# Attention with a mixture layer behind it: the normalised input of a batch's later groups goes through DRAM and is turned on VectorE, one group ahead

## The chip, the cores and the metric

The kernel runs on one core of one Trainium2 chip. The metric is the time on the device of one execution, in microseconds (us); the kernel before has a median of 1635.58 us over 3 runs. The core's engines each work through an instruction stream of their own, in order, and meet at semaphores: TensorE (PE, matrix products and transposes into PSUM), VectorE (DVE), ScalarE (ACT), GpSimd (POOL) and SyncE (SP, which here only issues DMAs). An engine that waits holds up all that stands behind the wait in its stream.

## The reference

Four batches of 2048 tokens of width 512, in float32. Attention with a layer norm of its own in front, a residual, a second layer norm, then a mixture layer and a third norm:

```
xn   = layernorm(x) * gamma + beta                    # per token
q, k, v = xn @ Wq, xn @ Wk, xn @ Wv                   # 512 x 512 each
p    = softmax(causal(q @ k.T / sqrt(512)))
x1   = layernorm(x + (p @ v @ Wo + x))
gates = the two largest of softmax(x1 @ wr.T), over their sum      # 8 experts
out[i] += gate * h      # h = silu(silu(x1 @ w1.T) @ w3.T) @ w2.T, added at rows 0 to 7
out  = layernorm(x1 + out)
```

## The kernel before

The weights are folded first: M = Wq·Wkᵀ and Wv·Wo, so that scores are (xn·M)·xnᵀ and the output projection is gone. Every product is made of three float32r products (hi·hi, lo·hi, hi·lo, in `split_product`, lines 351 to 353), which is why each operand exists twice, as `..._hi` (rounded by a copy) and `..._lo` (the rest, a subtraction on DVE).

A batch has 16 tiles of 128 tokens in 4 groups of 4 tiles. For tile t, PE computes the scores of tile t+1 against all keys so far (in chunks of 512 keys, one PSUM bank each), turns the probabilities of tile t, and multiplies them with V (`attend`). ACT takes the exponentials and rounds; DVE takes the maxima and the `lo` halves. In tiles 8 to 14 the probabilities are turned by way of DRAM: SP stores them (`store_p`) and loads them back 32 x 32 blocks at a time (`load_p`, four DMAs of 32 partitions each), and DVE finishes the turn inside the blocks. At the end of the third tile of a group (t % 4 = 2) PE projects the next group: V of its first tile, then G = xn·M (`project_g`), then V of its other three tiles. From the last tile of a batch on, the four loops run over into tile 0 of the next batch; the loop body goes from tile 7 of one batch to tile 6 of the next (`PEELED` = 7).

**The input.** Rows of x are loaded two tiles at a time (a pair) into one buffer `xin`, by ACT's queue; DVE takes their statistics (`norm_x`), POOL makes scale and shift of them, ACT applies these in place. PE then turns them: `turn_x(b, g, u)`, four units u a group, four 128 x 128 transposes each (line 1262). ACT applies gamma and beta on the way out of PSUM (`affine`, line 625), DVE makes `xt_hi` and `xt_lo` (`split_x`, lines 915 and 917). For groups 1 to 3 the units stand in the group before: u = 0 and 1 in its first tile, u = 2 and 3 in its third; for group 0 they stand in tiles 14 and 15 of the batch before.

**The token buffers.** `tok` has 4 slots. SP loads the rows of tile t for the residual; POOL doubles them, DVE adds the attention (`residual`), then two norms follow (`norm_behind`): ACT normalises tile t (x1), SP stores it (`store_x1(t)`, line 421), and only when that store has landed does ACT normalise the slot a second time in place; SP stores that to the output (`store_out`, line 425), and the slot is free for the load of tile t+4. The second normalisation of tile t-1 stands in ACT's stream right behind the first one of tile t, in these lines of `norm_behind`:

```
slot = (t - 1) % SLOTS
act.wait_ge(x1_stored[slot], (b * USES + (t - 1) // SLOTS + 1) * DMA)
y = tok[:, slot, :]
normalise(1, y, y).then_inc(out_ready, 1)
```

`norm_behind(b, 0)`, which stands at the end of ACT's tile 1, thus waits for the store of tile 15 of the batch before. SP's step t, in order: load `tok` of tile t; store and load probabilities (tiles 8 to 14); `store_x1(t-2)`; `store_out(t-3)`.

Of the kernel before, what the change touches and what calls it, by code (L numbers as in the profile page):

```python
# [30 lines left out]
P = 128  # L31
D = 512
# [8 lines left out]
def attention_mlp(nc, x, wq_t, wk_t, wv_t, wo, gamma, beta, w1_t, w3_t, w2_t, wr_t, out):  # L41
# [32 lines left out]
    x1_scratch = nc.dram_tensor("x1_scratch", [B * S, D], F32, kind="Internal").ap()  # L74

    with ExitStack() as whole:
# [44 lines left out]
        rinv = sb("rinv", [P, 2], F32, stage01)  # L121
        xt_hi = sb("xt_hi", [P, DC, S], F32R, stage01)
# [46 lines left out]
        x_loaded = [sem(f"x_loaded{i}") for i in range(2)]  # L169
        x_normed = sem("x_normed")  # L170
        x_turned = sem("x_turned")
# [210 lines left out]

        block = whole.enter_context(nc.Block())
# [9 lines left out]
        def _(sp):  # L393
            for s in start_at_one:
                sp.sem_inc(s, 1)
            weights = [w.rearrange("(c p) n -> p c n", p=P) for w in (wq_t, wk_t, wv_t, wo)]
            for pair in range(2):
                for part, c in enumerate(PARTS):
                    for i in (2 * pair, 2 * pair + 1):
                        sp.dma_start(raw[i][:, c, :], weights[i][:, c, :]).then_inc(weights_loaded[i][part], DMA)  # L400
                if pair == 0:
                    sp.dma_start(gamma_sb[:], gamma).then_inc(affine_loaded, DMA)
                    sp.dma_start(beta_sb[:], beta).then_inc(affine_loaded, DMA)
# [22 lines left out]

            def tile(b, t, before=True, last=False):
# [3 lines left out]
                sp.dma_start(tok[:, slot, :], x[bass.ds(b * S + t * P, P), :]).then_inc(res_loaded[slot], DMA)  # L431
                if t in FAR:
# [17 lines left out]
                if t in FAR:  # L450
                    for c in range(2, chunks(t)):
                        load_p(b, t, c)

            for t in range(3):
                tile(0, t, before=False)
            with sp.Fori(0, B - 1) as b:
                for t in range(3, TILES):
                    tile(b, t)
                for t in range(3):
                    tile(b + 1, t)  # L460
            for t in range(3, TILES):
# [27 lines left out]
        def _(pool):  # L489
# [26 lines left out]
            def norm_x(b, pair):  # L516
                n = b * PAIRS + pair
# [11 lines left out]
            def tile(b, t, last=False, before=True):  # L529
# [5 lines left out]
                if k == 3 and g + 2 < GROUPS:  # L535
                    norm_x(b, 2 * (g + 2))
                if k == 3 and g + 2 == GROUPS and not last:
                    norm_x(b + 1, 0)
# [8 lines left out]
                if t == TILES - 1 and not last:  # L547
                    norm_x(b + 1, 2)
                if k == 0 and g + 1 < GROUPS:
                    norm_x(b, 2 * (g + 1) + 1)  # L550
# [8 lines left out]
            for pair in range(FIRST_PAIRS):  # L559
                norm_x(0, pair)  # L560
# [40 lines left out]
        def _(act):  # L601
# [12 lines left out]
            def load_x(b, pair):  # L614
                for slot in range(2):
                    act.dma_start(xin[:, slot, :], x[bass.ds(b * S + (2 * pair + slot) * P, P), :]).then_inc(x_loaded[slot], DMA)

            def turn_x(b, g, u, more=True):

                n = g * XUNITS + u  # L620
                act.wait_ge(xt_ready, 1 + b * (GROUPS * XUNITS) + n)
                act.wait_ge(x_turned, b * (GROUPS * XUNITS) + n + 1)
# [5 lines left out]
                if u % 2 == 1 and more:  # L628

                    if n // 2 + 1 < TILES // 2:  # L630
                        load_x(b, n // 2 + 1)
                    else:
                        load_x(b + 1, 0)
# [9 lines left out]
            def norm_x(b, pair):  # L643
                act.wait_ge(x_shift, b * PAIRS + pair + 1)
                normalise(2, xin[:, 0, :], xin[:, 0, :])
                normalise(3, xin[:, 1, :], xin[:, 1, :]).then_inc(x_normed, 1)
# [62 lines left out]
            def tile(b, t, last=False, before=True):  # L709
# [5 lines left out]
                if more and k == 0:  # L715
                    turn_x(b, g + 1, 0)
                if chunks(t) > 1:
                    turn_probs(b, t, 1)
                if more and k == 0:
                    turn_x(b, g + 1, 1)  # L720
                if more and k == 2:
                    turn_x(b, g + 1, 2)
# [8 lines left out]
                if more and k == 1:  # L731
                    norm_x(b, 2 * (g + 1) + 1)
                for c in range(max(chunks(t), n_next)):
                    if c >= 2 and c < chunks(t):
                        turn_probs(b, t, c)
                    if more and k == 2 and c == chunks(t) - 1:
                        turn_x(b, g + 1, 3, more=not (last and g + 2 == GROUPS))
# [6 lines left out]
                    if c == 1 and t == TILES - 2 and not last:  # L744
                        turn_x(b + 1, 0, 1)
                    if c == 1 and t == TILES - 1 and not last:
                        turn_x(b + 1, 0, 3)
                    if c == 2 and t == TILES - 1 and not last:
                        project_g(b + 1, 0)
                if t == TILES - 2:  # L750
                    turn_probs(b, TILES - 1, 0)
                if k == 3 and g + 2 < GROUPS:
                    norm_x(b, 2 * (g + 2))
                if k == 3 and g + 2 == GROUPS and not last:
                    norm_x(b + 1, 0)
# [4 lines left out]
                if more and k == 2:  # L760
                    project_v(b, GROUP * (g + 1))
                    project_g(b, g + 1)
                    for j in range(1, GROUP):
                        project_v(b, GROUP * (g + 1) + j)
                if t == TILES - 1 and not last:
                    exp_first(b)
                    norm_x(b + 1, 2)
# [22 lines left out]
            load_x(0, 0)  # L790
            weights_to_hi(0, range(1))
            norm_x(0, 0)
            weights_to_hi(0, range(1, 2))
            act.wait_ge(affine_loaded, 2 * DMA)
            turn_x(0, 0, 0)
            weights_to_hi(0, range(2, 3))
            turn_x(0, 0, 1)
# [3 lines left out]
            norm_x(0, 1)  # L801
            turn_x(0, 0, 2)
            turn_x(0, 0, 3)
# [3 lines left out]
            norm_x(0, 2)  # L807
# [55 lines left out]
        def _(dve):  # L863
# [40 lines left out]
            def norm_x(b, pair):  # L904
                for s in range(2):
# [620 lines left out]
```

## Time and profile before

| | |
|---|---|
| median of 3 runs | 1635.58 us (1634.55 to 1635.96) |
| the profiled execution, its time | 1635.72 us |
| its span in the profile | 1633.9 us |
| busy: PE, DVE, ACT, POOL | 99%, 54%, 42%, 17% |
| granted TensorE clock | 1.00 throughout |
| DMA: SP's queue, ACT's queue | 28.5% and 3.6% of 16 engines' span |

How to read it: PE is the engine that counts, and its busy share is nearly the whole span, so time comes off only where PE has less to do, and goes on where something makes PE wait. The busy time of a group of PE instructions is the union of overlapping intervals; what one instruction costs is better read from the distance of the starts around it. Attention takes the first 1180 us or so, the mixture layer the rest; the change touches attention alone.

### The profile page before, as it was taken

How to read it: one execution, taken by the hardware profiler on the slowest of the kernel's cores; microseconds unless marked ns; L12 is line 12 of the kernel's file. 1: busy time of each engine (PE TensorE's matmuls, PEld its weight loads, DVE VectorE, ACT ScalarE, POOL GpSimd, SP SyncE). 2: the span in 40 equal slices, each digit the busy share in tenths (PEclk: the TensorE clock that was granted, in tenths of full speed). 3: DMA queues.
4: the chain of work that ended last, by engine and by line, in shares of the span. 5: the costliest groups of instructions: out<-in, count | busy, mean ns of one | idle time of the engine just before them, and what ended most of it. 6: DMA issues, size and time to landing. Idle time of an engine off the chain costs nothing.

```text
span 1633.9 us, 23601 instructions
## 1 busy us (share of the span) xinstructions
PE 1615.7 (99%) x7591; PEld 1335.6 (82%) x7591; DVE 885.7 (54%) x2296; ACT 681.0 (42%) x1301; POOL 283.8 (17%) x491
## 2 busy tenths in 40 slices
PE   9999999999999999999999999999999999999998
PEld 7888888888888888888888888888878888888886
DVE  5564645565364555455455545545565656556563
ACT  5443433353343344343333434343344444444442
POOL 1120201121120112121101212010131221212211
PEclk9999999999999999999999999999999999999999
DMA  4111625321154432123535123253664313223100
GB/s 161 59 61 52 155 76 139 100 94 56 60 136 104 113 94 95 54 91 107 134 85 123 61 76 104 78 138 97 157 133 63 51 26 51 37 40 51 26 0 8
DMA packets 365766, 136.64 MB, mean 84 GB/s; under 512 B 317008, under 2 KB 321104, under 8 KB 365664
## 3 DMA queue, kind: packets, MB, share of 16 engines
q1 hardware_dynamic: 354768, 116.48, 28.5%
q10 hardware_dynamic: 10896, 18.90, 3.6%
q8 instruction: 53, 0.87, 0.2%
q14 instruction: 49, 0.40, 0.1%
HBM read 79.73 MB, written 55.59 MB: 83 GB/s over the span
## 4 chain that ended last, share of the span: by engine, by line
PE 80%; issue 10%; DVE 4%; ACT 2%; POOL 2%; DMA 1%; ACTq 0%; POOLq 0%; SPq 0%; DVEq 0%
PE psum L351 25%; PE psum L353 25%; PE psum L352 25%; PE psum L1326 1%; PE psum L1262 1%; PE psum L1437 1%; PE psum L1436 1%; POOL rstd L512 1%; PE psum L1445 1%; PE psum L1444 1%; DVE pt_lo L934 1%; ACT affine L625 1%; ACT tok L641 0%; DMA raw<-in_wk_t 0%; DVE xt_hi L915 0%
## 5 line engine op out<-in xcount | busy, mean ns | idle before, releaser
L351 PE MATMUL psum<-xt_hi,g_hi 128*128 128x512 f32 (+3 forms) x640 | 237.5, 371 | 0.4 <-DVE g_lo L923 0.4
L353 PE MATMUL psum<-xt_lo,g_hi 128*128 128x512 f32 (+3 forms) x640 | 229.6, 359 | 0.0
L352 PE MATMUL psum<-xt_hi,g_lo 128*128 128x512 f32 (+3 forms) x640 | 229.3, 358 | 0.0
L351 PE MATMUL psum<-v_hi,pt_hi 128*128 128x512 f32 x544 | 220.8, 406 | 6.2 <-DVE pt_lo L934 3.9
L353 PE MATMUL psum<-v_lo,pt_hi 128*128 128x512 f32 x544 | 212.8, 391 | 0.0
L352 PE MATMUL psum<-v_hi,pt_lo 128*128 128x512 f32 x544 | 212.7, 391 | 0.0
L509 POOL TENSOR_TENSOR var_eps<-meanvar,eps 128x2 f32<-128x2 f32 (+1 forms) x97 | 18.9, 195 | 1005.4 <-DVE meanvar L901 1004.3
L946 DVE TENSOR_REDUCE rowmax<-psum 128x1 f32<-128x512 f32 (+3 forms) x160 | 97.1, 608 | 149.1 <-PE psum L353 147.7
L820 ACT ACTIVATE act_f<-psum 128x512 f32<-128x512 f32 x128 | 76.7, 599 | 199.7 <-PE psum L353 199.1
L641 ACT ACTIVATE tok<-tok,shift,rstd 128x512 f32<-128x512 f32 x128 | 97.5, 809 | 104.1 <-POOL shift L514 103.8
L590 POOL TENSOR_TENSOR expo<-euler,shifted 128x32 f32<-128x32 f32 x16 | 86.9, 5429 | 282.1 <-DVE shifted L1163 282.1
L696 ACT ACTIVATE pt_hi<-pt_f 128x512 fp32r<-128x512 f32 (+2 forms) x96 | 55.4, 578 | 191.0 <-DVE pt_f L942 190.4
L351 PEld LDWEIGHTS psum<-xt_hi,g_hi 128*128 128x128 f32 x640 | 121.1, 189 | 17.1 <-issue 0.7
L352 PEld LDWEIGHTS psum<-xt_hi,g_lo 128*128 128x128 f32 x640 | 120.7, 189 | 15.9
L353 PEld LDWEIGHTS psum<-xt_lo,g_hi 128*128 128x128 f32 x640 | 120.3, 188 | 15.9
L351 PEld LDWEIGHTS psum<-v_hi,pt_hi 128*128 128x128 f32 x544 | 102.2, 188 | 34.6 <-DVE pt_lo L934 11.3
L353 PEld LDWEIGHTS psum<-v_lo,pt_hi 128*128 128x128 f32 x544 | 102.2, 188 | 22.6
L352 PEld LDWEIGHTS psum<-v_hi,pt_lo 128*128 128x128 f32 x544 | 102.4, 188 | 18.3
L679 ACT ACTIVATE probs<-psum,bias 128x512 f32<-128x512 f32 (+3 forms) x157 | 97.1, 623 | 28.5 <-DVE bias L953 12.4
L927 DVE TENSOR_TENSOR v_lo<-psum,v_hi 128x512 fp32r<-128x512 f32 x64 | 44.1, 689 | 119.5 <-ACT v_hi L663 119.5
L923 DVE TENSOR_TENSOR g_lo<-psum,g_hi 128x512 fp32r<-128x512 f32 x64 | 44.3, 692 | 118.7 <-ACT g_hi L638 118.7
L351 PE MATMUL psum<-wvo_hi,h_hi 128*128 128x512 f32 x256 | 101.7, 397 | 2.0 <-DVE h_lo L1153 2.0
(149 smaller groups left out, 3400.6 us busy)
## 6 DMA issues: line engine op xcount, KB each, us to landing
xin<-in_x ACTq DMA_DIRECT2D x64, 256.0 KB, 2.8
tok<-in_x SPq DMA_DIRECT2D x64, 256.0 KB, 2.7
x_scratch<-tok SPq DMA_DIRECT2D x64, 256.0 KB, 2.2
out_dram<-tok SPq DMA_DIRECT2D x64, 256.0 KB, 2.3
p_scratch<-probs SPq DMA_DIRECT2D x64, 256.0 KB, 2.0
probs<-p_scratch SPq DMA_DIRECT2D x256, 64.0 KB, 2.5
x_in<-x_scratch SPq DMA_DIRECT2D x64, 256.0 KB, 4.3
p_scratch<-probs SPq DMA_DIRECT2D x16, 192.0 KB, 1.9
```

The lines of the kernel that those rows point to most:

```text
L351: pe.matmul(o, ws, ms, start=first, stop=False, skip_group_check=True)
L352: pe.matmul(o, w_lo, ms, start=False, stop=False, skip_group_check=True)
L353: return pe.matmul(o, ws, m_lo_, start=False, stop=last, skip_group_check=True)
L509: pool.tensor_tensor(var_eps[:, a:z], meanvar[:, a:z, 1], eps[:, o], ALU.add).then_inc(rooted, 1)
L590: pool.tensor_tensor(expo[:], euler[:], shifted[:], ALU.pow).then_inc(exp_ready, 1)
L641: return act.activation(o, y, ACT.Identity, bias=shift[:, slot:slot + 1], scale=rstd[:, slot:slot + 1])
L679: act.activation(probs[:, at:at + w], psum[:, c, 0:w], ACT.Exp, bias=bias[:, t % 2:t % 2 + 1], scale=SCALE, accum_out=sums4[:, t % 2, c:c ...
L696: act.activation(pt_hi[:, n % 2, 0:w], turned_, ACT.Copy).then_inc(pt_hi_ready, 1)
L820: act.activation(act_f[:, n % 2, :], psum[:, bank, :], ACT.Silu)
L923: dve.tensor_tensor(g_lo[:, j, :], psum[:, j, :], g_hi[:, j, :], ALU.subtract).then_inc(g_ready, 1)
L927: dve.tensor_tensor(v_lo[:, tile, :], psum[:, turn_bank(v_use(tile)), :], v_hi[:, tile, :], ALU.subtract).then_inc(v_ready, 1)
L946: return dve.tensor_reduce((rowmax if chunks(t) == 1 else rowmax4)[:, c:c + 1], psum[:, c, 0:width(t, c)], AX.X, ALU.max)
```

## The change

For groups 1 to 3 of batches 1 to 3, and for group 3 of the first batch (`in_dram`), PE no longer turns the input. ACT normalises a pair in place as before; SP stores the pair to a new DRAM buffer (`store_xn`), and one group ahead loads the whole group back in 32 x 32 blocks (`load_xq`: 16 DMAs of 32 partitions and 64 KB, four for each of the four blocks of 128 columns) into the memory of `xt_lo`, seen as unrounded floats (`xt_b`). DVE turns it inside the blocks into the memory of `xt_hi` (`turn_xq`, four transposes of 128 x 512), ACT applies gamma and beta into `xt_b` (`affine_x`), DVE makes `xt_hi` and `xt_lo` in place (`split_xq`). This stands under the projection of the group in front, between the `lo` half of its first V tile and those of G; for group 1 it stands in tile 15 of the batch before. The loads of group 2 stand in SP's step 1, those of group 3 at the end of step 5, those of the next batch's group 1 in step 15. The pairs of a batch are now normalised in the order 2, 3, 4, 0, 1, 5, 6, 7, mostly loaded by SP; in the first batch pairs 6 and 7 are loaded behind the weights into `xt_a`. Group 0, and groups 1 and 2 of the first batch, are turned by PE as before.

```
+        def in_dram(first, g):
+            return g >= (FIRST_PE_GROUPS if first else 1)        # FIRST_PE_GROUPS = 3
+            def store_xn(b, pair, first=False):
+                sp.wait_ge(x_normed, normed_before(b, pair, first) + 1)
+                sp.dma_start(pair_rows(xn_scratch, b, pair), x_pair(pair, first)).then_inc(xn_stored, DMA)
+            def next_pair(b, pair, behind):
+                sp.wait_ge(xn_stored, stored_with(b, behind) * DMA)
+                load_pair(sp, b, pair)
+            def load_xq(b, g):
+                rows_of = xn_scratch[bass.ds(b * S + g * (GROUP * P), GROUP * P), :].rearrange("(t j) (c q i) -> q j c t i", j=LANES, q=QUADRANTS, i=LANES)
+                for c in range(DC):
+                    for q in range(QUADRANTS):
+                        sp.dma_start(xt_b[q * LANES:(q + 1) * LANES, c, columns(g)].rearrange("j (t i) -> j t i", i=LANES),
+                                     rows_of[q][:, c]).then_inc(xq_loaded[g], DMA)
             def tile(b, t, before=True, last=False):                        # SP
                 sp.wait_ge(out_stored[slot], 1 + (b * USES + t // SLOTS) * DMA)
                 sp.dma_start(tok[:, slot, :], x[bass.ds(b * S + t * P, P), :]).then_inc(res_loaded[slot], DMA)
+                if t < PEELED and before:
+                    if t == 0:
+                        store_xn(b, 5)
+                    if t == 1:
+                        next_pair(b, 6, behind=5)
+                        load_xq(b, 2)
...
+                    if t == TILES - 1:
+                        sp.wait_ge(scores_ready, b * CHUNKS + CHUNKS)
+                        load_xq(b + 1, 1)
...
                 elif before:
                     store_x1(b - 1, TILES + t - 2)
...
+                if t == 5:
+                    sp.wait_ge(xn_stored, stored_with(b, 7) * DMA)
+                    load_xq(b, 3)
...
+            def affine_x(b, g, c):                                          # ACT
+                act.wait_ge(xq_turned, dram_groups_before(b, g) * DC + c + 1)
+                act.activation(xt_b[:, c, columns(g)], xt_a[:, c, columns(g)],
+                               ACT.Identity, bias=beta_sb[:, c:c + 1], scale=gamma_sb[:, c:c + 1]).then_inc(affine_ready, 1)
...
+            def turn_xq(b, g, c):                                           # DVE
+                dve.wait_ge(xq_loaded[g], (b + 1 if g == GROUPS - 1 else b) * (DC * LOADS))
+                dve.transpose(xt_a[:, c, columns(g)], xt_b[:, c, columns(g)]).then_inc(xq_turned, 1)
+            def split_xq(b, g, c):
+                n = (b * GROUPS + g) * XUNITS + c + 1
+                dve.wait_ge(affine_ready, 1 + n)
+                dve.tensor_copy(xt_hi[:, c, columns(g)], xt_b[:, c, columns(g)]).then_inc(xt_hi_ready, 1)
+                dve.wait_ge(xt_hi_ready, n)
+                dve.tensor_tensor(xt_lo[:, c, columns(g)], xt_b[:, c, columns(g)], xt_hi[:, c, columns(g)],
+                                  ALU.subtract).then_inc(xt_ready, 1)
...
                 if more and k == 2:                                         # DVE, end of a group's third tile
-                    split_x(b, g + 1, 3)
                     split_v(b, GROUP * (g + 1))
+                    if g + 2 < GROUPS and in_dram(not before, g + 2):
+                        for part in range(DC):
+                            turn_xq(b, g + 2, part)
+                        for part in range(DC):
+                            split_xq(b, g + 2, part)
                     split_g(b, g + 1)
```

Three places where the streams now read otherwise. The first is SP's step 1 of a later batch: the load of `tok` for tile 1, the store of x1 of tile 15 of the batch before, its `out` store of tile 14, and the wait for tile 2's slot. Before:

```order
L431 ISA [waits out_stored1]
L431 DMA tok<-in_x 128x512
L420 REGISTER_ALU
L421 DMA x_scratch<-tok 128x512 [waits x1_ready]
L425 DMA out_dram<-tok 128x512 [waits out_ready]
L431 ISA [waits out_stored2]
```

The same step now; the rows left out repeat the two of `xt_b` until there are 16 DMAs:

```order
L523 DMA tok<-in_x 128x512 [waits out_stored1]
L508 ISA
L435 ISA [waits xn_stored]
L435 DMA xin<-in_x 128x512
L435 ISA
L435 DMA xin<-in_x 128x512
L516 DMA xt_b<-xn_scratch 32x16x32
L516 ISA
...
L516 DMA xt_b<-xn_scratch 32x16x32
L496 REGISTER_ALU
L497 DMA x_scratch<-tok 128x512 [waits x1_ready]
L501 DMA out_dram<-tok 128x512 [waits out_ready]
```

Two loads of a pair and 16 block loads have come between the load of tile 1 and the store of x1 of tile 15.

The second is ACT from the end of tile 1 into tile 2 of a later batch: the first normalisation of tile 0, the second of tile 15 of the batch before, and the rounding of tile 2's turned probabilities (`pt_hi`), which PE's `attend` of tile 2 needs. Before:

```order
L641 ACTIVATE tok<-tok,shift,rstd 128x512 [waits shift_ready]
L657 ISA
L641 ACTIVATE tok<-tok,shift,rstd 128x512 [waits x1_stored3]
L693 REGISTER_ALU [waits probs_turned]
L696 ACTIVATE pt_hi<-psum 128x384 [waits pv_done]
L621 REGISTER_ALU
L625 ACTIVATE affine<-psum,beta_sb,gamma_sb 128x256 [waits x_turned,xt_ready]
```

And now:

```order
L770 ACTIVATE tok<-tok,shift,rstd 128x512 [waits shift_ready]
L787 REGISTER_ALU
L770 ACTIVATE tok<-tok,shift,rstd 128x512 [waits x1_stored3]
L823 REGISTER_ALU [waits probs_turned]
L826 ACTIVATE pt_hi<-psum 128x384 [waits pv_done]
L773 REGISTER_ALU
L770 ACTIVATE xin<-xin,shift,rstd 128x512 [waits x_shift]
```

The order of these is as it was up to `pt_hi`; behind it the `affine` of the input is gone and the normalisation of a pair has come.

The third is DVE at the projection in tile 2 of a later batch. Before:

```order
L927 TENSOR_TENSOR v_lo<-psum,v_hi 128x512 [waits v_hi_ready]
L914 REGISTER_ALU
L915 CAST xt_hi<-affine 128x2x256 [waits affine_ready]
L917 TENSOR_TENSOR xt_lo<-affine,xt_hi 128x2x256 [waits xt_hi_ready]
L927 TENSOR_TENSOR v_lo<-psum,v_hi 128x512 [waits v_hi_ready]
L923 TENSOR_TENSOR g_lo<-psum,g_hi 128x512 [waits g_hi_ready] x4
```

And now, with two more pairs of CAST and TENSOR_TENSOR in the rows left out:

```order
L1083 TENSOR_TENSOR v_lo<-psum,v_hi 128x512 [waits v_hi_ready] x2
L1055 STREAM_TRANSPOSE xt_a<-xt_b 128x512 [waits xq_loaded2] x4
L1059 ISA
L1060 CAST xt_hi<-xt_b 128x512 [waits affine_ready]
L1061 REGISTER_ALU
L1062 TENSOR_TENSOR xt_lo<-xt_b,xt_hi 128x512 [waits xt_hi_ready]
...
L1062 TENSOR_TENSOR xt_lo<-xt_b,xt_hi 128x512 [waits xt_hi_ready]
L1079 TENSOR_TENSOR g_lo<-psum,g_hi 128x512 [waits g_hi_ready]
```

Four transposes and four pairs of copy and subtraction now stand between V of the group's first tile and the `lo` half of G.

## Rows read from the trace of the kernel before

**Rows 1.** The page, part 1: busy time, share of span, instructions.
```profile
PE 1615.7 (99%) x7591; PEld 1335.6 (82%) x7591; DVE 885.7 (54%) x2296; ACT 681.0 (42%) x1301; POOL 283.8 (17%) x491
```

**Rows 2.** Grouped instructions, by form: op, tiles, count | busy us, mean ns | idle before.
```profile
L1262 PE MATMUL psum<-ident,xin 128*128 128x128 f32 x256 | 38.6, 273 | 1.5 <-ACT affine L625 1.0
...
L942 DVE STREAM_TRANSPOSE pt_f<-probs 128x512 f32<-128x512 f32 x64 | 45.1, 705 | 9.0 <-PE psum L353 9.0
L917 DVE TENSOR_TENSOR xt_lo<-affine,xt_hi 128x512 fp32r<-128x512 f32 x64 | 44.3, 692 | 2.2
...
L915 DVE CAST xt_hi<-affine 128x512 fp32r<-128x512 f32 x64 | 28.6, 447 | 24.0 <-ACT affine L625 23.7
```

**Rows 3.** Timeline of PE, tile 10: start us, us, line, op, [idle before].
```profile
203.00 0.60 PE L1262 MATMUL psum<-ident,xin 128*128 128x128 f32 x4
...
203.67 0.40 PE L352 MATMUL psum<-v_hi,pt_lo 128*128 128x512 f32 x1
203.90 0.40 PE L353 MATMUL psum<-v_lo,pt_hi 128*128 128x512 f32 x1
```

**Rows 4.** Timeline of PE, batch 1, tile 2: the turn, and attend.
```profile
354.81 0.55 PE L1326 MATMUL psum<-ident,probs 128*128 128x128 f32 x3 [0.15 <-ACT probs L679]
...
361.67 0.48 PE L351 MATMUL psum<-v_hi,pt_hi 128*128 128x512 f32 x1
```

**Rows 5.** Timeline of SP's DMA issues, batch 1, steps 0 and 1.
```profile
347.49 0.33 SPq L421 DMA_DIRECT2D x_scratch<-tok  x1
348.19 0.33 SPq L425 DMA_DIRECT2D out_dram<-tok  x1
350.34 0.35 SPq L431 DMA_DIRECT2D tok<-in_x  x1
351.49 0.33 SPq L421 DMA_DIRECT2D x_scratch<-tok  x1
```

**Rows 6.** Timeline of ACT, batch 1: norms in tiles 0 and 1.
```profile
346.66 1.51 ACT L641 ACTIVATE tok<-tok,shift,rstd 128x512 f32<-128x512 f32 x2
...
356.99 1.52 ACT L641 ACTIVATE tok<-tok,shift,rstd 128x512 f32<-128x512 f32 x2 [1.75 <-POOL shift L514]
```

**Rows 7.** Timeline of DVE, batch 1: tile 1's maximum, tile 2's probabilities.
```profile
344.65 0.42 DVE L946 TENSOR_REDUCE rowmax<-psum 128x1 f32<-128x256 f32 x1
...
358.91 0.56 DVE L934 TENSOR_TENSOR pt_lo<-psum,pt_hi 128x384 fp32r<-128x384 f32 x1 [2.20 <-ACT pt_hi L696]
```

**Rows 8.** Timeline of SP: eight block loads of 64 KB, four of 256 KB.
```profile
457.52 5.34 SPq L416 DMA_DIRECT2D probs<-p_scratch  x8
...
1183.27 5.11 SPq L361 DMA_DIRECT2D x_in<-x_scratch  x4
```

**Rows 9.** The page, part 6: DMA issues, KB each, us from issue to landing.
```profile
x_scratch<-tok SPq DMA_DIRECT2D x64, 256.0 KB, 2.2
...
probs<-p_scratch SPq DMA_DIRECT2D x256, 64.0 KB, 2.5
...
w_sb<-in_w_t SPq DMA_DIRECT2D x1, 1024.0 KB, 5.6
```

**Rows 10.** Timeline of DVE: idle in tile 15 (first two rows) and tile 6.
```profile
322.01 0.43 DVE L915 CAST xt_hi<-affine 128x512 fp32r<-128x512 f32 x1 [2.54 <-ACT affine L625]
...
328.30 0.69 DVE L923 TENSOR_TENSOR g_lo<-psum,g_hi 128x512 fp32r<-128x512 f32 x1 [3.08 <-ACT g_hi L638]
...
435.05 0.69 DVE L923 TENSOR_TENSOR g_lo<-psum,g_hi 128x512 fp32r<-128x512 f32 x1 [6.11 <-ACT g_hi L638]
```

**Rows 11.** Timeline of SP, batch 0: step 15 begins.
```profile
300.00 0.46 SPq L431 DMA_DIRECT2D tok<-in_x  x1
```

**Rows 12.** Stretch behind PE's last product: us, busy by engine (count), clock, DMA.
```profile
1629.00:1633.90 4.90, 0.00 (x0) 0.00 (x0) 2.20 (x5) 0.00 (x0) 0.55 (x1) 1.00 0.02 3
```

**Rows 13.** Grouped instructions of PE: products on the identity, early and late.
```profile
L1401 PE MATMUL psum<-ident 128*128 128x128 f32 x28 | 5.2, 368 | 2.3 <-POOL mask_bf L498 2.3
L1428 PE MATMUL psum<-ident 128*128 128x128 f32 x40 | 4.9, 277 | 0.1
```

More of the change, by code:

```diff
@@ L534, in tile @@
                 pool.tensor_tensor(y, y, y, ALU.add).then_inc(res_doubled, 1)
[L535 to L538, printed above, removed]
+                slot = pair_at(b, t, not before, last)
+                if slot and t in AT_MIDDLE:
+                    norm_x(*slot)
                 if t == TILES - 2 and not last:
@@ L559, in _ @@
             for pair in range(FIRST_PAIRS):
-                norm_x(0, pair)
+                norm_x(0, pair, first=True)
             for t in range(PEELED):
@@ L612, in fold_to_hi, with turn_x @@
                     act.activation((m_hi, wvo_hi)[pair][:, n % DC, :], psum[:, fold_bank(n), :], ACT.Copy).then_inc(fold_hi, 1)
[L614 to L622, printed above, removed]
+            def turn_x(b, g, u, first=False, then_load=None):
+                act.wait_ge(xt_ready, 1 + b * (GROUPS * XUNITS) + g * XUNITS + u)
+                act.wait_ge(x_turned, turned_before(b, g, u, first) + 1)
                 for k in range(2):
@@ L714, in tile @@
                     turn_probs(b, t, 0)
[L715 to L716 removed]
+                on_pe = not before and not in_dram(True, g + 1)
+                if on_pe and k == 0:
+                    turn_x(b, g + 1, 0, first=True)
                 if chunks(t) > 1:
                     turn_probs(b, t, 1)
[L719 to L722, printed above, removed]
+                if on_pe and k == 0:
+                    turn_x(b, g + 1, 1, first=True, then_load=2 * (g + 1) + 1)
+                if on_pe and k == 2:
+                    turn_x(b, g + 1, 2, first=True)
                 if t == TILES - 2 and not last:
@@ L730, in tile @@
                     norm_behind(b, t - 2)
-                if more and k == 1:
-                    norm_x(b, 2 * (g + 1) + 1)
+                slot = pair_at(b, t - 1, not before, last) if t else None
+                if slot and t - 1 in AT_END:
+                    norm_x(*slot)
                 for c in range(max(chunks(t), n_next)):
@@ L735, in tile @@
                         turn_probs(b, t, c)
-                    if more and k == 2 and c == chunks(t) - 1:
-                        turn_x(b, g + 1, 3, more=not (last and g + 2 == GROUPS))
+                    if on_pe and k == 2 and c == chunks(t) - 1:
+                        turn_x(b, g + 1, 3, first=True, then_load=2 * (g + 2) if g + 2 < FIRST_PE_GROUPS else None)
                     if c < n_next:
@@ L751, in tile @@
                     turn_probs(b, TILES - 1, 0)
[L752 to L755, printed above, removed]
+                slot = pair_at(b, t, not before, last)
+                if slot and t in AT_MIDDLE:
+                    norm_x(*slot)
                 if t and t < TILES - 2:
@@ L998, in tile @@
                     turn_probs(b, t, 1)
-                if more and k == 0:
+                on_pe = not before and not in_dram(True, g + 1)
+                slot = pair_at(b, t, not before, last)
+                if on_pe and k == 0:
                     split_x(b, g + 1, 0)
@@ L1036, in tile @@
                 if t == TILES - 1 and not last:
+                    for part in range(DC):
+                        turn_xq(b + 1, 1, part)
                     split_x(b + 1, 0, 3)
@@ L1049, in tile @@
                     split_probs(b, t, 3)
+                if t == TILES - 1 and not last:
+                    split_xq(b + 1, 1, 2)
+                    split_xq(b + 1, 1, 3)
                 if t == TILES - 2:
@@ L1055, in tile @@
                     split_wr()
+                if on_pe and k == 2:
+                    split_x(b, g + 1, 3)
                 if more and k == 2:
-                    split_x(b, g + 1, 3)
                     split_v(b, GROUP * (g + 1))
+                    if slot and t in AT_PROJECTION:
+                        norm_x(*slot)
+                    if g + 2 < GROUPS and in_dram(not before, g + 2):
+                        for part in range(DC):
+                            turn_xq(b, g + 2, part)
+                        for part in range(DC):
+                            split_xq(b, g + 2, part)
                     split_g(b, g + 1)
```

212 lines of the change are left out of this document (153 added, 59 removed).

## The prediction

> **What bounds the kernel now.** I read the page's first part first: PE is busy 99% of the span and no other engine over 54% [rows 1]. So a change pays by what it takes from PE's stream and costs by the time for which it makes PE wait; work on DVE, ACT or the DMA queues costs nothing until PE waits for it. Then the grouped instructions, for the operation that goes [rows 2]; then the timelines of PE, SP, ACT and DVE at the places where the new work lands, to see what waits last there. The second step decides this case: it is not the transposes that cost, nor the work that replaces them, but a store that ends up behind the new loads on SP.
>
> **What is removed from PE.** The transposes of the input come as 256 instructions [rows 2], 64 units of four. In the timeline a unit starts at 203.00 and the second product behind it at 203.67, where two products behind each other are 0.23 apart (203.67 to 203.90) [rows 3]: a unit costs 0.67 - 0.23 = 0.44 us. Ten groups leave PE (group 3 of the first batch, groups 1 to 3 of three batches), four units each: 40 x 0.44 = 17.6 us. PE also waits 0.15 us for ACT at 354.81 [rows 4], behind a pair's normalisation that is no longer in ACT's tile 1; three batches, 0.5 us. Gross gain 18.1 us.
>
> **What takes its place on DVE and ACT.** A group needs four transposes (0.705 each), four copies (0.447) and four subtractions (0.692) [rows 2], 7.4 us of DVE. In tiles 2 and 6 they stand under the projection, where DVE idles 6.11 us before the first part of G [rows 10]. The copies wait for ACT's four `affine_x`, at 0.76 us each as in ACT's norms [rows 6], which start one transpose later and stay ahead of DVE. So the first part of G is 1 to 2 us late on DVE; the next parts catch up (0.69 us of work every 1.36 us), and PE needs G only behind three V tiles, 36 products of 0.23, 8 us. Cost 0. Were that cover gone, each microsecond over 8 would cost three to seven in the whole. In tile 15 the transposes (2.8 us) fall into the 2.54 us of idle before 322.01 and two of the splits into the 3.08 us before 328.30 [rows 10]; PE works on the first half of G there. Cost 0 to 0.5 us in all; I take 0.
>
> **Whether the loads are there in time.** SP is done with tile 14 at 300.00 [rows 11], and the last scores have run. Sixteen loads of 64 KB follow. The nearest row is the block load of the probabilities, of the same shape: eight take SP 5.34 us, 0.667 each [rows 8], and land 2.5 us after issue [rows 9]. So group 1's loads take 10.7 us and are there by about 314; for the transposes to end by 322.0 DVE must begin at 319: 5 us to spare. The loads of step 5 have a whole tile to spare.
>
> **What the loads delay: the term that decides.** In step 1 the 16 loads stand ahead of `store_x1` of tile 15. ACT's stream ends tile 1 with the second normalisation of tile 15, which waits for that store to land; behind it stands `pt_hi` of tile 2, behind that on DVE `pt_lo`, and PE's `attend` of tile 2 waits for that. Before, the store is issued at 351.49 [rows 5], lands 2.2 us later [rows 9], and ACT asks at 356.99 [rows 6]: nobody waits. Now, on the axis of batch 1:
> - DVE's maximum for tile 1 at 344.65 [rows 7] stood behind two splits of the input; without them, and with PE's unit gone, it comes about 1.0 us sooner; ACT is rid of two pairs of `affine` and two DMA issues. I put the norm of 346.66 [rows 6] at 344.7, 2.0 sooner, and with it the three issues of [rows 5]: the output store at 346.2, the load of tile 1, which waits 2.15 us for it, at 348.4.
> - Two loads of a pair: the first block load at 349.4 to 349.6.
> - 16 x 0.667 = 10.7 us, and up to 0.75 each, 12.0 us, for the register instruction ahead of each: the store issued at 360.2 to 361.6.
> - It lands 2.2 us later; ACT's second normalisation takes half of 1.52, 0.76; from the end of that pair (356.99 + 1.52 = 358.51) to the end of `pt_lo` (358.91 + 0.56 = 359.47) are 0.96 [rows 6, 7]; I add 0.15 for PE to start. Sum 4.1: 364.3 to 365.7.
> - PE would be there at 361.67 [rows 4] less four units and the wait, 1.9: 359.75.
>
> So PE waits 4.5 to 5.9 us, three times. The middle, 5.2, leaves out that the store's packets go behind block loads; I take 5.4: 16.2 us. Behind it nothing more is late: the delayed V halves, `exp` and the load of tile 2 have the projection's 22 us (96 products of 0.23). Step 5 puts the same loads ahead of `store_x1` of tile 4, which ACT needs only at the end of its tile 6, when two tiles' scores have passed: 0; if they were too short, each microsecond short would cost four. In step 15 the stores behind the loads wait for a norm in the middle of tile 15 anyway: 0. The bounds for this term: nothing (if SP gets through its 16 issues in under 6 us) to 3 x 8 (issues of 0.83).
>
> **The rest.** In the first batch two loads of 512 KB go behind the weights; a load of 1 MB lands in 5.6 us [rows 9], and ACT's second pair shares the engines with it: 0 to 3 us, I take 0.5. The pair stores and loads at SP's steps 8 to 12 add about 1 us to a step; the stores of probabilities behind them wait for ACT's exponentials that long: 0 to 1, I take 0.
>
> **The sum.** The profiled execution took 1635.7 us (the median of the runs is 1635.6). 1635.7 - 18.1 + 16.2 + 0.5 + 0 = 1634.3. By its own steps the forecast lies between 1629 and 1640.
>
> **Rivals.**
> 1. *SP gets through the loads quickly.* The x1 loads of the mixture layer move 1 MB with four issues in 5.11 us [rows 8]; if the time goes with the bytes and not with the issues, the 16 take 5.1 us, the store lands before 357, and PE waits for nothing: 1635.7 - 18.1 + 0.5 = 1618. Against it: the row of equal shape has 0.667 for 64 KB. The Trainium skill (DMA: Bandwidth & Descriptors, section "Issuing engines are not separate DMA queues") says the sequencer's time to start a DMA is usually small beside the DMA itself. By that rule the answer would be this rival's; the trace does not agree here, where 0.667 us an issue stands against 2.5 us to landing, and 16 issues are four times a landing.
> 2. *The wait also costs PE its clock* (the one on the slower side). If a wait of over 5 us lets TensorE fall to its lower level, PE starts `attend` of tile 2 slow. The price from rows: the program's first 14 products on the identity (28 records), after an idle start, took 5.2 us, and 20 of them late in the program (40 records) 4.9 us [rows 13]; 14 at the late rate are 3.4, so 1.8 us a time, 5.4 in three: 1639.7. It decides from the point where the wait outlasts what the clock holds. For it: the length. Against it: behind PE's last product the granted clock stays 1.00 over 4.90 us without one [rows 12], and the waits are only somewhat longer. The Trainium skill (TensorE: Matmul & The Clock Gate, section "What's actually happening") has activity as what releases the lower clock of 1.2 GHz and idleness as what brings it back; the row shows no fall within its 4.90 us.
> 3. *The block loads are slow*, at 1 us an issue, because 16 behind each other fill the queue: PE then waits 11 us in tile 2, and the loads of tile 15 land at 319, just in time: 1635.7 - 18.1 + 3 x 10.7 + 0.5 = 1650. Eight and even twelve such loads in one step do not slow down now, which speaks against it.
>
> **Chances.** Forecast 0.47, rival 1 0.18, rival 2 0.25, rival 3 and what I have not seen 0.10. A difference of less than about 0.2%, 3.3 us (1632.3 to 1638.9), is what a measurement of this kernel cannot tell from no change. The forecast's own spread of 5 us to both sides gives it about 0.13 faster, 0.29 the same, 0.05 slower; rival 1 is 0.18 faster; rival 2 0.08 the same and 0.17 slower; rival 3 0.02 the same and 0.08 slower. Together 0.31 faster, 0.39 the same, 0.30 slower. The range reaches from just over rival 1 to past rival 2: 1619 to 1645.
>
> **What would show it.** Right: in PE's waits three waits of 4 to 7 us before `attend` of tile 2 in batches 1 to 3, for `pt_lo`; ACT idle as long before a normalisation of `tok`, released by the DMA of x1; SP's 16 block loads in 10 to 12 us right before that store; the transposes on the identity down from 256 to 96; no wait of PE for `xt_lo` or `g_lo` at the projections. Wrong: SP through the loads in under 6 us and no wait (rival 1); the clock below 1.00 behind those waits (rival 2); waits in tile 15 or at the projections, which would put the cost in the loads or DVE instead.

## The result and the profile after

The changed kernel takes 1642.46 us (median of 8 runs, 1638.87 to 1648.61) against 1636.14 us before (8 runs, 1634.55 to 1637.51): a ratio of 1.0041, with a 95% interval from 1.0028 to 1.0054. It is slower by 6.3 us. I had forecast 1634.3 us, no change, with a chance of 0.30 for slower. The profiled execution is the slowest of the eight, 1648.61 us, with a mean granted clock of 0.992; the other seven have 0.994 to 0.996 and the kernel before 1.00. The sizes below that rest on the clock are therefore taken from several profiles and from the timed runs, not from this one alone. As an estimate, one less the mean clock, times the span, is the most that the half clock can have cost: 13 us in the profiled run, 7 to 10 in the other seven. In each set of experiments the kernel before was run again (medians 1636.21 to 1636.52), and the ratios are to these runs.

The page's first part and the grouped instructions answer to [rows 1, 2]. The transposes of the input on PE are 96 where 256 were, and the 40 transposes on DVE take 0.679 us each, where 0.705 was forecast:

```profile
PE 1609.1 (98%) x7431; PEld 1329.1 (81%) x7431; DVE 906.6 (55%) x2336; ACT 671.5 (41%) x1261; POOL 280.9 (17%) x491
...
L1433 PE MATMUL psum<-ident,xin 128*128 128x128 f32 x96 | 14.5, 273 | 0.8 <-ACT affine L752 0.8
...
L1055 DVE STREAM_TRANSPOSE xt_a<-xt_b 128x512 f32<-128x512 f32 x40 | 24.8, 679 | 0.0
```

The first thing to look at is what PE waits for (us in total, times, longest). One line has grown. Before:

```profile
PE psum L351 <- DVE pt_lo L934: 3.9, 9, 1.4
```

And now:

```profile
PE psum L360 <- DVE pt_lo L1090: 22.1, 13, 4.0
```

PE's timeline shows where these 22.1 us lie. Three waits stand before `attend` of tile 2 (367.65, and 3.89 and 3.81 us in the next two batches), as the prediction has them, 11.7 us together. Another 6.8 us stand in places that the prediction does not have: in `attend` of tile 9 (191.39, 490.08, 493.53, 787.10) and once in that of tile 8 (776.48); the last batch, which prepares no input, has none of them. (The tile is told by its products, three for each tile of keys: 30 follow in tile 9. The expectations below say tiles 9 and 10.) The other 3.7 us lie in places where the kernel before waits too. There is no new wait at the projections or in tile 15:

```profile
191.39 0.47 PE L360 MATMUL psum<-v_hi,pt_hi 128*128 128x512 f32 x1 [1.96 <-DVE pt_lo L1090]
...
367.65 0.77 PE L360 MATMUL psum<-v_hi,pt_hi 128*128 128x512 f32 x1 [3.97 <-DVE pt_lo L1090]
...
369.06 0.63 PE L360 MATMUL psum<-v_hi,pt_hi 128*128 128x512 f32 x1
...
490.08 0.47 PE L360 MATMUL psum<-v_hi,pt_hi 128*128 128x512 f32 x1 [2.16 <-DVE pt_lo L1090]
```

The row at 369.06 shows a second loss: three products take 1.41 us there (367.65 to 369.06) where 0.69 (3 x 0.23) is what they take elsewhere. The windows around the wait (us; busy us of PE, PEld, DVE, ACT, POOL; granted clock; DMA) show the clock at its lower level behind it:

```profile
360.00:364.00 4.00, 3.67 (x17) 2.68 (x15) 0.44 (x1) 0.08 (x1) 1.12 (x4) 1.00 0.81 128
364.00:368.00 4.00, 0.35 (x1) 0.38 (x2) 1.06 (x2) 2.28 (x4) 0.00 (x0) 0.83 0.51 155
368.00:372.00 4.00, 4.00 (x10) 3.09 (x10) 2.58 (x10) 1.58 (x4) 2.23 (x5) 0.50 0.84 307
372.00:376.00 4.00, 4.00 (x16) 3.18 (x15) 0.00 (x0) 2.06 (x3) 1.09 (x2) 0.81 0.50 145
```

The wait itself is followed back over SP and ACT (they answer to [rows 5, 6]). The store of x1, at 351.49 before, is issued at 363.05, behind 16 block loads; ACT's second normalisation waits 5.65 us for its landing:

```profile
353.02 0.88 SPq L435 DMA_DIRECT2D xin<-in_x  x2
354.00 8.82 SPq L516 DMA_DIRECT2D xt_b<-xn_scratch  x16
363.05 0.38 SPq L497 DMA_DIRECT2D x_scratch<-tok  x1
```

```profile
365.72 0.81 ACT L770 ACTIVATE tok<-tok,shift,rstd 128x512 f32<-128x512 f32 x1 [5.65 <-DMA x_scratch<-tok]
366.44 0.47 ACT L826 ACTIVATE pt_hi<-psum 128x384 fp32r<-128x384 f32 x1
```

The waits of tile 9 begin on SP too. In the kernel before, SP issues the load of `tok` in step 9, waits for ACT's probabilities, stores them, and loads them back from 179.12 on:

```profile
173.10 0.45 SPq L431 DMA_DIRECT2D tok<-in_x  x1
176.69 2.28 SPq L408 DMA_DIRECT2D p_scratch<-probs  x3
179.12 5.37 SPq L416 DMA_DIRECT2D probs<-p_scratch  x8
```

Now SP stands from 176.34 to 180.10 until the stored pair has landed; only then does it issue the next pair's loads and, behind them, the stores of tile 9's probabilities. From the load of `tok` to the first block load are 8.4 us instead of 6.0, and DVE gets the probabilities back too late by the 2.46 us of the last row:

```profile
175.30 0.46 SPq L505 DMA_DIRECT2D xn_scratch<-xin  x1
175.97 0.37 SPq L523 DMA_DIRECT2D tok<-in_x  x1
180.10 0.87 SPq L435 DMA_DIRECT2D xin<-in_x  x2
181.09 1.37 SPq L484 DMA_DIRECT2D p_scratch<-probs  x3
184.40 5.36 SPq L492 DMA_DIRECT2D probs<-p_scratch  x8
```

```profile
189.07 0.71 DVE L1098 STREAM_TRANSPOSE pt_f<-probs 128x512 f32<-128x512 f32 x1 [2.46 <-DMA probs<-p_scratch]
```

In SP's waits the same shows as a new line, 20.0 us in nine waits (steps 3, 9 and 11 of three batches); in DVE's, the wait for the probabilities' loads is 12.8 us in nine where it was 1.1 in one:

```profile
SPq L435 <- DMA xn_scratch<-xin: 20.0, 9, 3.8
```

```profile
DVE pt_f L1098 <- DMA probs<-p_scratch: 12.8, 9, 2.5
```

In step 11 SP waits as long (from 208.28 to 212.10 in the first batch), but PE projects the next group ahead of `attend` of tile 11 and waits for nothing there.

### The profile page after: what moved, and what is told of

It reads as the page before. It is cut to its first block, busy times and chain, and to the rows that moved or that the text cites. A ratio compares the mean times of both kernels' runs of the same rounds, so it can differ in the third digit from the quotient of the medians.

```text
span 1646.8 us, 23816 instructions
## 1 busy us (share of the span) xinstructions
PE 1609.1 (98%) x7431; PEld 1329.1 (81%) x7431; DVE 906.6 (55%) x2336; ACT 671.5 (41%) x1261; POOL 280.9 (17%) x491
## 4 chain that ended last, share of the span: by engine, by line
PE 76%; issue 11%; DMA 3%; DVE 3%; SPq 2%; POOL 2%; ACT 2%; POOLq 0%; DVEq 0%; ACTq 0%
PE psum L360 24%; PE psum L362 24%; PE psum L361 24%; SPq L492 2%; DMA p_scratch<-probs 1%; PE psum L1497 1%; DMA xn_scratch<-xin 1%; POOL rstd L645 1%; PE psum L1610 1%; PE psum L1611 1%; PE psum L1619 1%; PE psum L1618 1%; ACT tok L770 1%; DMA raw<-in_wk_t 1%; PE psum L1433 1%
## 5 line engine op out<-in xcount | busy, mean ns | idle before, releaser
L360 PE MATMUL psum<-v_hi,pt_hi 128*128 128x512 f32 x544 | 222.2, 408 | 25.0 <-DVE pt_lo L1090 22.1
L360 PEld LDWEIGHTS psum<-xt_hi,g_hi 128*128 128x128 f32 x640 | 121.1, 189 | 17.6 <-issue 0.8
L360 PE MATMUL psum<-wvo_hi,xt_hi 128*128 128x512 f32 x256 | 101.0, 395 | 0.0
```

The lines of the kernel that those rows point to most:

```text
L360: pe.matmul(o, ws, ms, start=first, stop=False, skip_group_check=True)
```

## The experiments

The theory after the two traces: the gain on PE is there; it is given back by two orders on SP (block loads ahead of the store of x1 in step 1; a wait for the stored pair ahead of the probabilities in steps 9 and 11), by the granted clock behind the waits, and by 1 to 2 us at the start. The rivals: the pair's loads, not the block loads, are the delay in step 1; contention between the transfers; DVE's new work. Each edit shown below is against the changed kernel.

**Stores first in step 1.**
```
                     if t == 1:
                         next_pair(b, 6, behind=5)
-                        load_xq(b, 2)
...
+                if t == 1 and before:
+                    load_xq(b, 2)
                 if t == 2 and before:
                     store_xn(b, 6)
```


> Alone of the changed kernel: in SP's step 1 the 16 block loads go behind the stores of that step. Theory (the loads ahead of the store of x1 make PE wait, and the clock falls behind the wait): the three waits of 3.8 to 4.0 us before attend of tile 2 go, 11.7 us, and with them three stretches of 6.8 us at half clock, up to 10 us; 1620 to 1626, and a mean granted clock nearer to 1. Rival A (the two loads of a pair and the wait for the stored pair ahead of them are the delay): the waits lose less than 1 us each; 1639 to 1642. Rival B (the loss lies in DVE's work or in the transfers' contention): the waits stay or move; 1638 to 1643.

Measured: 1625.06 us (1623.56 to 1626.5), 0.9928 of before [0.9915, 0.9941], 17.4 us less than with the change as it was. The three waits are gone, and the mean clock is 0.999. What is left of the same line, 7.9 us, lies in tile 9 (0.98, 1.25 and 1.94 us in the three batches) and in places that waited before:

```profile
PE psum L360 <- DVE pt_lo L1091: 7.9, 8, 1.9
```

Neither contention nor DVE's work can be the main loss: the same bytes move and DVE does the same work.

**The pair later.**
```
                     if t == 1:
-                        next_pair(b, 6, behind=5)
+                        sp.wait_ge(xn_stored, stored_with(b, 5) * DMA)
                         load_xq(b, 2)
...
+                if t == 1 and before:
+                    load_pair(sp, b, 6)
```


> Alone of the changed kernel: in SP's step 1 the two loads of a pair go behind the stores of that step; the 16 block loads stay ahead of them. Theory: the store of x1 is about 1 us earlier, the three waits are 2.9 us instead of 3.9; 1637 to 1642, the clock may still fall. Rival A (the pair is the delay): the waits go, 1620 to 1626.

Measured: 1648.07 us (1646.55 to 1651.16), ratio 1.0074 [1.0060, 1.0089]: 5.6 us slower than the change, where I expected 1637 to 1642; neither the theory nor the rival has this. The waits of PE are 5.59, 6.24 and 5.41 us. The store of x1 does come earlier (359.32, 9.0 us behind the start of the step's first issue, the load of `tok`, where it was 10.7), and ACT is done with tile 2's `pt_hi` at 362.80. But now DVE is late: the statistics of pair 6 stand ahead of the residual and of `pt_lo`, and start at 364.37, when the pair's loads, now issued from 360.41 on, have landed (the view names no releaser for this wait):

```profile
364.37 1.29 DVE L1037 BATCH_NORM_STATS2 stats<-xin 128x6 f32<-128x512 f32 x2 [8.11 <-issue]
...
366.49 0.55 DVE L1092 TENSOR_TENSOR pt_lo<-psum,pt_hi 128x384 fp32r<-128x384 f32 x1
```

So two paths from SP's step 1 end in the same wait: over the store and ACT, and over the pair's loads and DVE. The pair's loads were not what delayed the store, but they are not free to go last either. Of the two, only the 16 block loads can go last in step 1.

**Pair loads behind the stores of the probabilities (steps 9 and 11).**
```
-                    if t == 9:
-                        next_pair(b + 1, 3, behind=2)
-                    if t == 11:
-                        next_pair(b + 1, 4, behind=3)
...
                     for c in range(chunks(t)):
                         store_p(b, t, c)
+                    if t in (9, 11) and not last:
+                        next_pair(b + 1, {9: 3, 11: 4}[t], behind={9: 2, 11: 3}[t])
                     for c in range(2):
                         load_p(b, t, c)
```


> Alone of the changed kernel: in SP's steps 9 and 11 the wait for the stored pair and the loads of the next pair go between the stores of the probabilities and their loads. Theory (SP's wait of 4 us holds up the probabilities): PE's waits in tiles 9 and 10 (1.96 us in the first batch, 2.61 in the second, 2.19 in the third) go or fall under 0.5, and the fall of the clock near 192 with them; 1633 to 1638. Rival (the pairs' stores and loads share the DMA engines with the probabilities, whatever the order): the waits stay; 1640 to 1643.

Measured: 1634.08 us (12 runs, 1631.5 to 1638.3), ratio 0.9987 [0.9978, 0.9996], 8.4 us less than the change. No wait over 0.3 us is left in tiles 8 to 10. SP's timeline (to be held against the one from 175.30 above; this run is about 1.3 us earlier by then) shows why. The three stores of probabilities are spread over 3.62 us, because SP waits for ACT between them; by then the pair has landed, and its successor's loads follow without a wait. The eight block loads start at 180.41 instead of 184.40, 2.7 us sooner when the 1.3 are taken off:

```profile
173.98 0.46 SPq L505 DMA_DIRECT2D xn_scratch<-xin  x1
174.65 0.37 SPq L523 DMA_DIRECT2D tok<-in_x  x1
175.49 3.62 SPq L484 DMA_DIRECT2D p_scratch<-probs  x3
179.41 0.88 SPq L435 DMA_DIRECT2D xin<-in_x  x2
180.41 5.34 SPq L492 DMA_DIRECT2D probs<-p_scratch  x8
```

Of SP's nine waits for a stored pair three are left, those of step 3:

```profile
SPq L435 <- DMA xn_scratch<-xin: 1.9, 3, 0.6
```

DVE still waits for the pair (2.59 us at 182.83, where it was 2.26), and PE does not wait for it. The transfers are the same, so contention whatever the order is out as the main loss here as well. In the change the first store of probabilities, right behind the pair's loads, did land late (issued at 181.09, its block loads could start only at 184.40); how much of the wait that made is not separated from SP's own wait.

**All three edits**, with the early loads of the first batch held back behind `sp.wait_ge(x_normed, 2)`.

> Both edits (stores first in step 1; pair loads behind the stores of the probabilities in steps 9 and 11), and the first batch's two early loads of 512 KB held until the second pair of the input is normalised. Theory: the gains add up, 18 to 22 us, 5 to 8 us and 0 to 1.5 us: 1613 to 1620, faster than the kernel before by 1.0 to 1.4%; no PE wait over 1.5 us but those that stand in the kernel before too. Rival (the gain of 17.6 us on PE is not there, because something else replaces the transposes): 1630 to 1636.

Measured: 1616.11 us (1615.39 to 1617.76), ratio 0.9875 [0.9860, 0.9889]: 20 us faster than the kernel before. PE's waits for `pt_lo` are down to what they were before the change (3.9 us in 9):

```profile
PE psum L360 <- DVE pt_lo L1089: 3.7, 5, 1.3
```

**The start.** The held-back loads alone, and the two other edits without them:

> Alone of the changed kernel: the two early loads of 512 KB are held until the second pair of the input is normalised. Theory (they and the longer start delay the weights and the second pair): the first scores start at 45.8 to 46.5 us instead of 48.2; 1639 to 1642. Rival (the start varies from run to run, whatever the loads): first scores at 46.8 to 48.3 as in the kernels with the early loads; 1641 to 1644.

Measured: 1643.01 us (1641.64 to 1644.67), no change; first scores at 47.31 us (the product behind PE's wait for the first `g_lo`). That is the rival's case.

> Stores first in step 1, and pair loads behind the stores of the probabilities in steps 9 and 11, with the early loads where the change put them. Theory: 1 to 2 us over the 1616.1 of the kernel with the early loads held back; 1616 to 1619, first scores at 46.8 to 48.3. Rival (holding back the early loads is worth nothing): 1615 to 1617.

Measured: 1617.91 us (1617.4 to 1618.65), ratio 0.9887 [0.9872, 0.9903]; first scores at 47.32 us. The start is settled in part only. When the first weights let PE begin varies from 7.7 to 9.96 us in all these profiles, whatever the loads. From there to the first scores it takes 38.4 to 39.1 us in seven of the eight profiles with the early loads (48.23 - 9.49 in the change), 40.5 in the eighth, and 37.4 to 38.2 in the three without (45.92 - 7.71 before). So the loads cost about 1 us, too little for the time of a single pair of kernels to show; the difference of 1.8 us between the two last versions, whose intervals overlap, fits it, and the first edit alone does not contradict it.

**The clock.** Ahead of `attend` of tile 2, PE works on the identity while it waits:
```
+                    if t == 2 and before:
+                        for _ in range(14):
+                            pe.matmul(psum[:, XBANK, 0:P], ident[:], ident[:], start=True, stop=True)
                     attend(b, t, c)
```


> Alone of the changed kernel: 14 products on the identity, about 3.4 us, into a bank that nobody reads, ahead of attend of tile 2 in batches 1 to 3, where PE waits 3.9 us anyway. The wait on DVE is not shortened. Theory (the clock falls behind the waits and that costs about 3 us a time): the waits left are about 0.5 us, the granted clock there stays 1.00; 1633 to 1638. Rival (the clock costs nothing beside the wait): no change, 1641 to 1644.

Measured: 1639.9 us (1636.75 to 1645.27), ratio 1.0030 [1.0018, 1.0042]: 2.6 us less than the change, under the 4 to 9 that I expected, and by itself not clear of the noise: the interval overlaps that of the change (1.0028 to 1.0054). PE's waits left behind the idle products are 0.93 to 1.28 us, where I expected 0.5. The clock holds:

```profile
360.00:364.00 4.00, 4.00 (x30) 3.68 (x29) 0.00 (x0) 0.00 (x0) 0.00 (x0) 1.00 0.77 198
364.00:368.00 4.00, 2.99 (x18) 2.50 (x17) 2.20 (x7) 3.87 (x7) 0.00 (x0) 1.00 0.50 133
```

The same on top of the kernel with the pair loads behind the stores of the probabilities, where no other wait blurs it:

> The kernel with the pair loads behind the stores of the probabilities (1634.1 us), with the 14 idle products ahead of attend of tile 2 besides, so that no wait in the far tiles blurs the price of the clock. Theory: of the 16.2 us by which that kernel is slower than the one with the stores first in step 1 as well (1617.9), three waits of 3.6 us are 10.8 and the clock is 5.4; with the clock held 1628 to 1631. Rival (the clock costs nothing beside the waits): 1633 to 1636.

Measured: 1632.6 us (11 runs, 1630.38 to 1635.46), ratio 0.9979 [0.9970, 0.9988]: 1.5 us less than without, short of the 3 to 6 expected, and again with overlapping intervals. The clock did hold in every run: its mean is 0.999 to 1.00 in all 11, where it is 0.994 to 0.997 in the 12 without the idle products. The profiles tell why so little came of it. Without the idle products the clock is low behind the wait:

```profile
362.00:366.00 4.00, 3.85 (x10) 3.07 (x11) 3.08 (x10) 2.08 (x5) 0.00 (x0) 0.57 0.66 232
```

The wait there is 3.56 to 3.64 us and tile 2's batch is 5.2 to 5.4 us longer than with the stores first (first `attend` of tile 15 to the next: 293.25, 293.00 and 291.46 against 287.83, 287.78 and 286.10). From the start of the last product to `attend` are 3.95 to 4.02 us there, 3.7 to 3.8 more than the usual 0.23, which leaves 1.5 to 1.6 us a time for the clock. With the idle products the batches are 4.4 to 5.0 longer, all of it wait: from the first idle product to `attend` are 4.4 to 4.9 us, 0.6 to 1.1 more than the 3.7 to 3.8 without them. In the first two of the three the store of x1 took 1.12 and 1.19 us to issue instead of 0.37, in the third the 16 block loads took 9.95 us instead of 8.84, so the store landed later. The clock's price, 1.5 to 1.6 us a time, is thus read from the profiles; the timed runs agree with it but do not fix it. Why SP was slower with PE busy, or whether that is chance, stays open.

**A quarter of the bytes.** In step 1 each block load is cut in two, a quarter of the rows ahead of the stores, three quarters behind:
```
                     if t == 1:
                         next_pair(b, 6, behind=5)
-                        load_xq(b, 2)
+                        load_xq(b, 2, slice(0, 1))
...
+                if t == 1 and before:
+                    load_xq(b, 2, slice(1, GROUP))
```


> Alone of the changed kernel: in step 1 each of the 16 block loads is cut in two: a quarter of it stays ahead of the store of x1, the other three quarters go behind the stores. 16 issues stay ahead, with a quarter of the bytes. If SP's time goes with the issues (0.55 us each), the waits before attend of tile 2 stay 3.9 us; 1640 to 1644. If it goes with the bytes or the rows, 16 issues take 3 to 6 us, the waits fall to 0 to 1.2 us, the clock holds; 1622 to 1630.

Measured: 1644.1 us (1642.81 to 1645.8), ratio 1.0047 [1.0032, 1.0063]. SP's time goes mainly with the number of issues:

```profile
353.50 7.90 SPq L516 DMA_DIRECT2D xt_b<-xn_scratch  x16
361.63 0.37 SPq L497 DMA_DIRECT2D x_scratch<-tok  x1
...
362.98 9.07 SPq L516 DMA_DIRECT2D xt_b<-xn_scratch  x16
```

16 quarters take 7.90 us, 0.49 each; 16 whole ones 8.82. The waits of tile 2 are 2.40 to 2.47 us, between the two expectations: 0.9 is from the issues, 0.6 because the store lands sooner (ACT has it 2.0 us after its issue, 2.7 in the change), probably for having fewer bytes ahead of it. What that saves comes back at the end of tile 2, where PE waits 1.43 to 2.19 us for `v_lo`. SP's load of `tok` for tile 2 now stands behind the second 16 loads and is issued at 372.24 instead of 366.54; POOL waits for it, ACT's next norm waits for POOL, and behind that norm stands the rounding of V:

```profile
372.24 0.35 SPq L523 DMA_DIRECT2D tok<-in_x  x1
```

```profile
377.61 1.52 ACT L772 ACTIVATE tok<-tok,shift,rstd 128x512 f32<-128x512 f32 x2 [10.07 <-POOL shift L649]
```

## Why the prediction was wrong

Four versions split the loss: 1616.11 (all three edits), 1617.91 (early loads back, +1.8), 1625.06 (pair loads back ahead of the probabilities, +7.2), 1642.46 (block loads back ahead of the store, +17.4). The other way round step 1 is worth 16.2 (1634.08 - 1617.91) and the pair loads 8.4 (1642.46 - 1634.08).

- *The gain on PE, 18.1 us:* about right, 2 us too small. From the first scores to the last batch's tile 15 the kernel before takes 1147.87 us (45.92 to 1193.79), the one with two edits 1127.76 (47.32 to 1175.08): 20.1. The price of a unit holds: in 39 of the 64 units of the kernel before, the second product behind a unit starts 0.67 or 0.68 us after it, as in the one place that I read. Laid side by side, the two PE streams differ by 18.1 us at the 40 units, near the 17.6 forecast; the other 2.0 us lie in many small steps between them, among them 0.3 us three times at the wait for ACT at 354.81, for which I had 0.15.
- *DVE and ACT under the projections and in tile 15, 0 us:* right. PE waits for neither `xt_lo` nor, there, `g_lo`. *The loads of tile 15 and step 5:* right, too.
- *The wait before `attend` of tile 2, 16.2 us:* the place, the chain and the count are right. That the sum is right as well is luck, for it is not made of what I added up. The wait is 3.6 to 4.0 us and not 5.4, because an issue takes SP 0.55 us there and not 0.667 to 0.75 [rows 8] (with the stores first the same 16 loads take 10.94 us, 0.68 each; why the two differ stays open). The rest is the clock, which this term did not have.
- *The clock (rival 2):* its mechanism is what happened, on top of a shorter wait than I had given it. I argued against it from 4.90 us without a fall behind PE's last product [rows 12]; before `attend` of tile 2 it fell with every wait of 3.56 us or more, twelve in four profiles. Its price, 1.8 a time, is near the 1.5 to 1.6 of the kernel with the pair loads moved; in the profile of the change itself it is higher, since the clock is low for longer there (the windows from 364 to 376 show 0.83, 0.50 and 0.81, where the other kernel has one window at 0.57).
- *Rival 1 (the bytes, not the issues):* wrong. The quarters show it. The rule of the Trainium skill that I weighed there (DMA: Bandwidth & Descriptors, section "Issuing engines are not separate DMA queues"), that the sequencer's time for a DMA is usually small beside the transfer, does not help here: 16 times 0.49 to 0.55 us stands ahead of a store that lands in under 3.
- *The pair stores and loads at SP's steps 8 to 12, "0 to 1, I take 0":* this is the step that failed, by 7.2 to 8.4 us. I counted the issues, about 1 us a step, and not the wait for the stored pair's landing ahead of the next pair's loads, 3.8 us at the place shown. My reason for 0, that the stores of probabilities wait for ACT that long, I read off no row. In the kernel before SP does wait there, from 173.55 to 176.69, which would cover the issues but not the wait besides; and in the kernel with the pair loads moved ACT is ready sooner, and SP waits for it only until 175.49, 0.5 us behind the load of `tok`. The 8.4 is the less certain of the two sizes: in the profiles the low clock behind tile 2's wait also lasts less long once the pair loads have moved.
- *The start, 0.5 us:* about 1 by the profiles, 1.8 by the two medians.

By my own terms: 1635.7 - 20.1 + 24.6 (16.2 + 8.4, or 17.4 + 7.2) + 1 to 1.8 gives 1641.2 to 1642.0, where 1642.46 was measured. The 24.6 is itself a difference of two measured times, so this sum tests the gain and the start alone.

## What to carry to other kernels

When a queue takes on a step, price its waits as well as its issues, and for each go through what stands behind it: the time that the next transfer has in hand has to be read off a row, not assumed. Put a wait for a landing where the queue has to wait in any case, and bulk loads behind the small stores that a chain needs. A wait of PE can cost more than its length, by the clock behind it: here 3.6 us of wait cost 5.2 to 5.4.

## What was not expected of the hardware

A wait's length alone did not decide whether the granted clock fell. It fell behind 1.96 us at 191.39 in the change (0.70 from 191 to 195):

```profile
191.00:195.00 4.00, 3.61 (x11) 2.96 (x12) 2.63 (x8) 2.41 (x4) 0.00 (x0) 0.70 0.62 175
```

In the same profile it held behind 2.16 us at 490.08:

```profile
494.00:498.00 4.00, 4.00 (x20) 3.28 (x19) 2.36 (x8) 2.02 (x7) 0.44 (x3) 1.00 0.66 242
```

It held behind 2.35 us at 190.86 in the kernel with the early loads held back alone, and fell with the wait of 2.40 us that ends at 365.60 in the kernel with the quarters. The first of these:

```profile
192.00:196.00 4.00, 4.00 (x19) 3.15 (x18) 2.29 (x9) 4.00 (x10) 0.00 (x0) 1.00 0.52 148
```

The Trainium skill (TensorE: Matmul & The Clock Gate, section "What's actually happening") has the clock set by how busy PE has been recently, and says of the slow start of a kernel that it varies from run to run. The waits of about 2 us above fit a dependence on more than the one wait, but no run here shows what decides them. Behind the waits of 0.48 and 1.48 us at the head of the mixture layer, which stand in the kernel before as well, the profile of the change shows a fall that the profile before does not: from tile 15 to the end it takes 441.8 us against 440.1. Six of the ten profiles of changed kernels show this fall, and some runs of the kernel before have a mean clock of 0.999 rather than 1.00, so it may come there too. Up to 1.7 us of a difference between two times can be this and not an edit.
